# Wide cross attention: keys projected for four sequences at once, and the projections moved right behind the scores

## The reference

```
q = jnp.einsum('bne,ef->bnf', x, wq)      # x: 128 tokens x 160, normalized; f = 1280
k = jnp.einsum('bme,ef->bmf', ctx, wk)    # ctx: 77 tokens x 96
v = jnp.einsum('bme,ef->bmf', ctx, wv)
scores = jnp.einsum('bhnd,bhmd->bhnm', q, k) * SCALE    # 20 heads of 64
attn = jax.nn.softmax(scores, axis=-1)
out = jnp.einsum('bhnm,bhmd->bhnd', attn, v)
return jnp.einsum('bnf,fe->bne', out, wo) + bo
```

## Time and profile before

| | us |
|---|---|
| median of 3 runs | 3719.72 |
| lowest, highest run | 3706.51, 3859.67 |
| the profiled execution | 3714.61 |
| its span, first to last instruction | 3712.8 |
| mean granted clock of PE, as a share of 2.4 GHz | 0.989 |

### The profile page before, as it was taken

How to read it: one execution, slowest core, us unless ns; L and a number is a source line. 1 busy time by engine, 2 the same in 40 slices (tenths; PEclk the granted TensorE clock), 3 DMA queues, 4 the chain that set the end, 5 groups by cost and what they waited for, 6 DMA issues and landing times. The chain is left out here.

```text
span 3712.8 us, 98282 instructions
## 1 busy us (share of the span) xinstructions
PE 3613.0 (97%) x38023; PEld 3125.9 (84%) x38023; DVE 2301.5 (62%) x3916; ACT 2091.5 (56%) x5165; POOL 1260.7 (34%) x1279
## 2 busy tenths in 40 slices
PE   5999999999999999999999999899999999999999
PEld 4777777877887889889899888788888888888888
DVE  2788866665454666666666666556555555556554
ACT  2677777775344655555555555455555555555333
POOL 4333333332442333333333333333233322333442
PEclk8899999999999999999999999999999999999999
DMA  4343433321101000000000000100000000000000
GB/s 112 91 100 86 105 80 85 91 76 50 43 0 35 2 1 0 0 0 0 0 0 0 0 0 1 25 3 2 2 2 1 2 2 2 1 2 1 19 19 25
DMA packets 99546, 98.72 MB, mean 27 GB/s; under 512 B 31248, under 2 KB 74128, under 8 KB 99344
## 3 DMA queue, kind: packets, MB, share of 16 engines
q1 hardware_dynamic: 94224, 94.50, 9.8%
q0 software_dynamic: 5120, 1.35, 0.2%
HBM read 20.76 MB, written 5.24 MB: 7 GB/s over the span
## 5 line engine op out<-in xcount | busy, mean ns | idle before, releaser
L1181 POOL TENSOR_TENSOR a_probs<-a_probs,a_rsums 128x1024 f32<-128x1024 f32 x160 | 303.5, 1897 | 752.8 <-DVE a_rsums L1306 752.8
L1219 ACT ACTIVATE a_probs<-a_scores_banks,a_negmax 128x128 f32<-128x128 f32 x1280 | 366.7, 376 | 284.6 <-DVE a_negmax L1294 284.5
L1181 POOL TENSOR_TENSOR c_probs<-c_probs,c_rsums 128x616 f32<-128x616 f32 x160 | 204.2, 1276 | 758.2 <-DVE c_rsums L1306 758.2
L704 ACT ACTIVATE s_probs<-s_scoresT_banks 128x1024 f32<-128x1024 f32 (+1 forms) x320 | 327.2, 1022 | 194.3 <-PE s_scoresT_banks L877 192.1
L1219 ACT ACTIVATE c_probs<-c_scores_banks,c_negmax 128x77 f32<-128x77 f32 x1280 | 312.2, 334 | 197.4 <-DVE c_negmax L1294 197.3
L789 DVE TENSOR_REDUCE s_negmax<-s_scores_banks 128x8 f32<-128x1024 f32 (+1 forms) x320 | 322.4, 1007 | 150.2 <-PE s_scores_banks L859 146.2
L1287 DVE COPY c_outT<-c_out_bank 128x512 f32<-128x512 f32 x160 | 110.7, 692 | 367.1 <-PE c_out_bank L1466 307.0
L1287 DVE COPY a_outT<-a_out_bank 128x512 f32<-128x512 f32 x160 | 110.7, 692 | 293.1 <-PE a_out_bank L1466 239.9
L1635 DVE SCALAR_TENSOR_TENSOR f_hidden<-f_value_bank,bias,f_gate 128x512 f32<-128x512 f32 x160 | 120.1, 751 | 244.9 <-ACT f_gate L1610 243.0
L667 POOL DMA_DIRECT2D s_q_stack<-s_shift x160 | 93.5, 585 | 504.7 <-ACT s_shift L727 498.6
L1294 DVE TENSOR_REDUCE a_negmax<-a_scores_banks 128x4 f32<-128x512 f32 x320 | 206.2, 686 | 88.2 <-PE a_scores_banks L1365 88.2
(11 more groups left out here) (308 smaller groups left out, 10613.9 us busy)
## 6 DMA issues: line engine op xcount, KB each, us to landing
s_q_stack<-front SPq DMA_DIRECT2D x192, 160.0 KB, 3.3
s_k_stack<-front SPq DMA_DIRECT2D x96, 160.0 KB, 3.7
s_out<-s_heads SPq DMA_DIRECT2D x128, 80.0 KB, 2.5
s_k_stack<-front SPq DMA_DIRECT2D x96, 96.2 KB, 2.8
x_tokens<-in_x SPq DMA_DIRECT2D x16, 320.0 KB, 4.7
out_x<-x_tokens SPq DMA_DIRECT2D x16, 320.0 KB, 2.4
s_q_stack<-s_shift POOLq DMA_DIRECT2D x160, 8.0 KB, 2.7
s_ctx_in<-in_ctx SPq DMA_DIRECT2D x16, 115.5 KB
```

The costliest lines, as they stand in the source:

```text
L704: nc.scalar.activation(probs[i][0:NK, :, :], scoresT[0:NK, :, :], ACT.Exp).then_inc(s_exp, 1)
L1181: nc.gpsimd.tensor_tensor(probs[i][:], probs[i][:], rsums[(k - 1) % 2][:].unsqueeze(2).broadcast_to([P, UNIT, NK]), ALU.mult).then_inc(s_p ...
L1219: done = nc.scalar.activation(probs[i][:, h, :], scores[:, h // GROUP, h % GROUP * NK:(h % GROUP + 1) * NK], ACT.Exp, bias=negmax[k % 2][: ...
```

## The change

In `c1` alone:

- The keys get a tensor of their own, `keys_two`, 308 columns (4 x 77) per tile for the four sequences of a double. One tile of 128 rows is projected by three matmuls of 308 columns, once per double; before, the same tile was projected twice, by three matmuls of 154 columns for each pair.
- `KEY_TILES` says in which step which of the ten key tiles of the next double is projected: one tile in k = 6, 8, 9, 0, 2, 3, two tiles in k = 7 and k = 1, none in k = 4 and 5. All go through `odd_bank`.
- Both query tiles of a step go into `even_bank` (2 x 256 columns), and ACT copies them in one instruction of 512 columns (`query_out`).
- PE does the queries and keys right behind the scores (and the transposes of the norm), ahead of `transpose_step`; the values stay where they were, behind `output_step`.
- ACT does four exponentials, the query copy, four exponentials, the key copies (`keys_out`), the value copy.
- The context is transposed, cast and split once per double, for four sequences, in step k = 5: four transposes on PE right behind the scores, `ctx_high` of 308 columns at the head of ACT's step, `ctx_low` of 308 columns at the head of DVE's step. Its two loads are issued together in k = 0.

```
+        KEY_TILES = {6: (0,), 7: (1, 2), 8: (3,), 9: (4,), 0: (5,), 1: (6, 7), 2: (8,), 3: (9,)}
...
+        def keys_at(q, k):
+            double = q + (k + GROUPS) // BODY
+            return [(t, double, double * TILES + t) for t in KEY_TILES.get(k % BODY, ())] if cross and live(double, QUADS) else []
...
+            def query_out(q, k):
...
+                    act.wait_ge(s_qkproj, r + 1)
+                    nc.scalar.copy(qk[:, 2 * g:2 * g + 2, :], even_bank[:].rearrange("p (t n) -> p t n", t=2)).then_inc(s_qk, 1)
+
+            def keys_out(q, k):
+                for t, double, order in keys_at(q, k):
+                    act.wait_ge(s_kproj, order + 1)
+                    nc.scalar.copy(keys_two[:, t, :], odd_bank[:, 0:QUAD * NK]).then_inc(s_k, 1)
...
-                exponentials(q, k, 0, 6)
-                tile_out(q, k, 0)
-                exponentials(q, k, 6, 8)
-                tile_out(q, k, 1)
+                double = both_at(q, k)
+                if k == GROUPS and double is not None:
+                    act.wait_ge(crossing.s_T, 2 * double + 2)
+                    act.wait_ge(s_vproj, BODY * double)
+                    nc.scalar.copy(ctx_high[0:CTX_D, :], odd_bank[0:CTX_D, 0:QUAD * NKC]).then_inc(crossing.s_high, 2)
+                if cross:
+                    exponentials(q, k, 0, 4)
+                    query_out(q, k)
+                    exponentials(q, k, 4, 8)
+                    keys_out(q, k)
...
+                double = both_at(q, k)
+                if k == GROUPS and double is not None:
+                    dve.wait_ge(crossing.s_high, 2 * double + 2)
+                    nc.vector.tensor_tensor(ctx_low[0:CTX_D, :], odd_bank[0:CTX_D, 0:QUAD * NKC],
+                                            ctx_high[0:CTX_D, :].bitcast(F32), ALU.subtract).then_inc(s_ctx_split, 2)
                 if live(n - Y_LAG, WUNITS):
...
+            def project_queries(q, k):
...
+                if due(r):
+                    pe.wait_ge(s_v, r)
...
+                for i in range(2):
+                    cols = slice((2 * g + i) * P, (2 * g + i + 1) * P)
+                    last = products(nc, even_bank[:, i * KCOL:(i + 1) * KCOL],
+                                    [(qh[:, cols], hh), (qh[:, cols], hl), (ql[:, cols], hh), (qs[0:STACK, cols], hs)])
+                last.then_inc(s_qkproj, 1)
+
+            def project_keys(q, k):
+                for i, (t, double, order) in enumerate(keys_at(q, k)):
+                    if due(order):
+                        pe.wait_ge(s_k, order)
+                    if i == 0 and k % BODY in (3, 8):
+                        pe.wait_ge(done.s_y, 2 * (BASE + capped(pair_of(q, k) + 3, PAIRS)))
+                    if t == 0:
+                        pe.wait_ge(s_ctx_split, 2 * double + 2)
...
+                    products(nc, odd_bank[:, 0:QUAD * NK],
+                             [(kh[0:CTX_D, cols], ch), (kh[0:CTX_D, cols], cl), (kl[0:CTX_D, cols], ch)]).then_inc(s_kproj, 1)
+
+            def project_values(q, k):
...
+                pe.wait_ge(s_qk, r + 1 if cross else 2 * r + 1)
...
+                if cross:
+                    project_queries(q, k)
+                    project_keys(q, k)
                 transpose_step(q, k - T_LAG)
                 output_step(q, k - Y_LAG)
-                project(q, k, 0)
-                project(q, k, 1)
+                if not cross:
+                    project(q, k, 0)
+                    project(q, k, 1)
                 project_values(q, k)
                 values_step(q, k - T_LAG)
```

More of the change, by code:

```diff
@@ L463, in __init__ @@
         self.ctx_in = [sb(f"ctx_in{i}", [P, PAIR, CTX_D]) for i in range(2)]
-        self.high = [sb(f"ctx_high{i}", [P, PAIR * CTX_TOK], F32R) for i in range(2)]
-        self.low = [sb(f"ctx_low{i}", [P, PAIR * CTX_TOK], F32R) for i in range(2)]
+        self.high = sb("ctx_high", [P, QUAD * CTX_TOK], F32R)
+        self.low = sb("ctx_low", [P, QUAD * CTX_TOK], F32R)
         self.s_in = [m.semaphore(f"ctx_in{i}") for i in range(2)]
@@ L1074, in attention_wide @@
         s_qk = sem("qk_ready")
+        s_kproj = sem("kproj")
+        s_k = sem("k_ready")
         s_vproj = sem("vproj")
@@ L1364, in scores_step @@
                             rows, t, col = slice(dh * j, dh * j + dh), 2 * g + c, (2 * c + a) * NK
-                            last = nc.tensor.matmul(scores[:, j, col:col + NK], qk[rows, t, a * P:(a + 1) * P],
-                                                    qk[rows, t, KCOL + a * NK:KCOL + (a + 1) * NK], start=True, stop=True)
+                            if cross:
+                                keys = keys_two[rows, t, (k // GROUPS * PAIR + a) * NK:(k // GROUPS * PAIR + a + 1) * NK]
+                            else:
+                                keys = qk[rows, t, KCOL + a * NK:KCOL + (a + 1) * NK]
+                            last = nc.tensor.matmul(scores[:, j, col:col + NK], qk[rows, t, a * P:(a + 1) * P], keys,
+                                                    start=True, stop=True)
                 last.then_inc(s_scores, 1)
@@ L1490, in step @@
                     last.then_inc(crossing.s_T, 1)
+                double = both_at(q, k)
+                if k == GROUPS and double is not None:
+                    pe.wait_ge(s_k, TILES * double)
+                    for i in range(2):
+                        pe.wait_ge(crossing.s_in[i], 16 * (double + 1))
+                        for a in range(PAIR):
+                            last = nc.tensor.transpose(odd_bank[0:CTX_D, (i * PAIR + a) * NKC:(i * PAIR + a + 1) * NKC],
+                                                       crossing.ctx_in[i][0:NKC, a, :], m.ident[0:NKC, 0:NKC])
+                    last.then_inc(crossing.s_T, 2)
+                if cross:
+                    project_queries(q, k)
+                    project_keys(q, k)
                 transpose_step(q, k - T_LAG)
                 output_step(q, k - Y_LAG)
-                project(q, k, 0)
-                project(q, k, 1)
+                if not cross:
+                    project(q, k, 0)
+                    project(q, k, 1)
                 project_values(q, k)
```

84 lines of the change are left out of this document (52 added, 32 removed).

## The result

The changed kernel is slower: 3785.57 us in the median of five runs (3769.71 to 3835.72), beside 3741.65 for the kernel before on the same chip (3706.51 to 3859.67). The two medians also hold executions that a lower clock made longer; without those over 1.5% above the fastest of their kernel (one of five on either side) the ratio is 1.0167, 95% interval [1.0117, 1.0218]: about 62 us, 43 to 81, where +36 was forecast. That is slower beyond doubt, while a loss of 2% is neither shown nor excluded. The median lies inside the range of the forecast, near its upper end of 3792.

What follows compares the result with a forecast made beforehand. PE was taken to bound stage c1 (busy 198.4 of 200 us). Terms -19 - 12 - 6 + 53 + 8 + 12 = +36 us on 3714.6 gave 3750.6; predicted 3752 us, range 3718 to 3792.

Steps and rivals of the forecast that it cites:

- PE's own work: Queries and keys on PE in c1: 0.12 us saved per step over 155 steps, -19 us (ends -9 and -26).
- `ctx_low` wait gone: In s = 4 the odd bank no longer waits for `ctx_low`: 0.39 us in 30 pairs, -12 us.
- values' wait in s = 3 gone: In s = 3 the values no longer wait for the even copy: 0.2 us x 30, -6 us.
- second key tile: In k = 7 and k = 1 PE waits for ACT's copy of the first tile: 31 x 1.72 = +53 us (47 to 62).
- k = 3 and k = 8: Key tile waits for ACT's norm passes on the odd bank: 0.27 us in 30 steps, +8 us (0 to 12).
- k = 5: DVE waits for ACT's `ctx_high` ahead of `outT` and maxima, delaying the values: 15 x 0.8 = +12 us (8 to 18).
- falls of the clock: Rival: PE's clock falls behind the new waits, 1.5 us each; all 31 give +47 us, 3799; chance 0.10 of enough for 2%.
- its case of a third of the waits: A third of the 31 long waits draw a clock fall: 3768 us; chance of a third or so 0.17.
- the second tile hardly waits: Rival: ACT's first key copy is done early, wait under 0.55 us; with none 3698, or 3703 by the median; chance 0.06.
- the third: Rival: PE's savings at their upper end, small waits don't come: -26 - 12 - 6 + 50 = +6, 3721 us; chance 0.12.
- What was counted as hidden: Query copy (1.0 us of cover or more), key copy, ACT's copying per step and context loads: counted at nothing.
- The signs named in the prediction: In the changed trace: 1.7 us extra between key tiles 31 times, PE share about 94%, c1's granted clock 1.00, among others.

Runs made afterwards that it cites:

- all_three: Changed kernel, second key tiles and key tiles of k = 3, 8 behind the output projection, DVE's `ctx_low` behind the maxima; ratio 0.9915 to kernel before.
- context_later: Changed kernel with DVE's `ctx_low` in k = 5 moved behind `outT` and the maxima; c1 1113.6 us, against 1128.4 changed.
- filled_wait: Changed kernel with 14 idle matmuls of 256 columns ahead of the second key tile, keeping PE busy in the wait; c1 1104.2 us.
- all_three_narrow: all_three with each key tile projected by two times three matmuls of 154 columns; c1 1049.0 us, ratio 1.0016 to kernel before.
- move_alone: Kernel before with its projections moved behind the scores and transposes of norm and context, `ctx_low` behind the maxima; c1 1071.2 us, against 1058.9.
- late_second: Changed kernel with the second key tile of k = 1 and 7 behind the output projection; c1 1046.1 us, ratio 1.0013 to kernel before.
- early_copy: Changed kernel with ACT's copy of the first of two key tiles ahead of the last four exponentials; c1 1074.6 us.
- wide_old_place: Changed kernel with queries and keys put back behind the output projection, ahead of the values; c1 1193.8 us, 3865.53 in all.

## Why the prediction was wrong in its size

The sign and the places were right, and the size was short by half. The working's terms for c1 beside what the steps show:

| term | forecast, us | measured, us | from |
|---|---|---|---|
| PE's own work | -19 | -24 | one-tile steps 6.32 for 6.475 |
| `ctx_low` wait gone | -12 | -12 | k = 4 takes 5.89 = 6.32 less a tile, no wait in it |
| values' wait in s = 3 gone | -6 | -6 | no row of it is left |
| second key tile | +53 | +62 | 31 x (8.74 - 6.32 - 0.43) |
| k = 3 and k = 8 | +8 | +10 | all_three: 0.35 x 30 |
| k = 5 | +12 | +15 | context_later: 1.0 x 15 |
| sum without falls | +36 | +45 | |
| falls of the clock | 0 (a rival) | +24 | filled_wait |
| sum | +36 | +69 | c1: +69.5 |

The terms come out this near to c1 with some help: the 6.8 us fall in c1's first steps, worth 2.8, is in none of them, so the others are 2 or 3 us too high in sum.

**PE's work** came out at -0.155 a step, between the middle and the upper end of the prediction's range. all_three_narrow and move_alone say whence: from the width, not from the place. These 5 us more than forecast hid as much of what the waits and the clock cost beyond it.

**The second key tile is the term that was mis-sized.** The cause was right: late_second removes it, early_copy shortens it by what ACT's queue gives. The prediction had 1.72 from PE's readiness to its restart. Measured from the start of the scores, PE is ready at 2.54 (2.57 forecast); the first exponential starts at 1.76 (1.69), the key copy at 3.91 (3.82), and it takes 0.47, not 0.42; PE restarts at 4.44 (4.29), a wait of 1.90. The first matmul behind a pause then costs 0.10 more, a slow start that the prediction knew from its other terms and left out here. Together 1.99, against 1.72: +9 us with rounding, and at the upper end (2.0) of the bounds.

**The clock is the step that failed.** The prediction took c1's clock as 1.00 and kept the falls for a rival, on one pair of rows: no fall behind idle 1.74, a fall behind 1.88. That read as a threshold just above its own wait. There is none: in c1's body the same wait, 1.67 to 1.75 idle, drew a fall in 15 of 30 cases. The waits at the end of a1, which the change leaves alone, come out otherwise in the changed kernel's own trace than in the earlier trace rows. Timeline of PE there:

```profile
2381.60 1.09 PE L1546 MATMUL a_out_bank<-a_probsT,a_v 128*64 128x128 f32 x16 [1.88 <-DVE a_probsT L1355]
2382.63 1.16 PE L1418 MATMUL a_scores_banks<-a_qk 64*128 64x128 f32 x16
...
2387.64 1.09 PE L1546 MATMUL a_out_bank<-a_probsT,a_v 128*64 128x128 f32 x16 [1.75 <-DVE a_probsT L1355]
2388.67 1.99 PE L1418 MATMUL a_scores_banks<-a_qk 64*128 64x128 f32 x16
```

Behind 1.88 the scores take 1.16 here, behind 1.75 they take 1.99. Two rows of one execution that differ by 0.14 us can't tell a limit from chance. The rival's price of 1.5 us was right (1.6 measured); its case of a third of the waits, +16 us, came nearest, and it was half of them, +24. Had half the falls been in the forecast, it would have given 3752 + 24 = 3776, and with the longer wait 3785. The prediction's reason for few falls, three or more dense steps between two waits, is refuted: dense work ahead of the pause did not prevent a fall. The Trainium skill (TensorE: Matmul & The Clock Gate, Part 1) has the throttled clock as the default and activity as what releases it. The trace agrees that activity matters: filled_wait, with PE busy in the same 2.05 us, has no fall in the 30 steps that it fills.

**Small slips in the working.** By its own terms the forecast of the median is 3719.7 + 36 = 3756, not 3752. The cover of the query copy in a step with no key tile is 4.04 - 3.17 = 0.87 us, not 1.0 or more. Neither bears on the outcome. And its 1.72 us is counted from PE's readiness, while the 1.74 and 1.88 of the earlier trace rows are the profile's idle times, in which the measured wait of 1.90 shows as 1.75; set beside them, 1.72 was a longer wait than it should have been.

**k = 3, k = 8 and k = 5** are short by the same slow start and by 0.1 to 0.2 us of ACT and DVE: 0.35 and 1.0 instead of 0.27 and 0.8.

**The other rivals.** That the second tile hardly waits is refuted (wait 1.90, it needed under 0.55). Of the third, PE's savings nearly reached their upper end (-24 for -26), but the small waits came. What was counted as hidden stayed so: in steps with one key tile no wait for the query copy, the key copies or the context loads is seen, and wide_old_place shows what the cover is worth.

**The signs named in the prediction** came: two starts of key tiles 2.05 us apart (1.85 forecast), released by `c_keys`; PE's share at 93% (94%); 0.14 to 0.25 idle before the keys in k = 3 and 8 (0.3 forecast); the values of k = 5 released by `c_qk`. Two were wrong: the granted clock in c1, at 0.97 the sign named for its failure, and by a little the length of the wait.

## What to carry to other kernels

Where two producers fill one bank in turn, the second waits for the consumer's whole queue: count what stands there ahead of the copy, and put the second producer behind other work of its engine (moving three matmuls down in two of ten steps gave 82 us here). On an engine that bounds the kernel, price a wait of about 1.4 us or more, in this kernel, as the wait, plus the slow restart, plus a share of clock falls; don't read a limit for these from two rows. An edit that saves work per instruction should be tried apart from the reordering that comes with it: here the width was worth 29 us, and the place, tried by itself, cost 12.

## What the runs showed of the hardware

- The same wait of PE, 1.67 to 1.75 us idle in a dense stream, is followed by 1.2 GHz in 15 of 30 cases of c1's body and by 2.4 GHz in 15, in one execution of the changed kernel. Which ones differs between executions that differ in other steps only (context_later). Idle 1.43 drew one in 14 of 30 in wide_old_place, where PE also waits shortly in most other steps. Idle 0.80 to 0.88 drew none in 31 (early_copy), and neither did the long wait filled with matmuls.
- Short pauses in close order did draw one: at the start of c1 in early_copy, eight pauses of 0.25 to 0.85 us in some 14 us, none longer, end in a fall at 2375.7. What decides between fall and none is open.
- The fall doesn't show at once, and not always at the same place: 0.35 us after the restart in k = 1 of the changed kernel, 1.5 in k = 7, 0.7 to 2.1 in wide_old_place. So the slow work can stand well behind the wait.
- The falls have different lengths: 3.4 us in the body of the changed kernel, 6.8 in wide_old_place and at c1's start, and 102 in s0, where work that is the same in all these kernels ran at 0.93 on average in two executions (changed, all_three) and at 1.00 in the others. What sets the length is open.
- A matmul of 154 columns has 0.105 us to itself in a row of its kind, one of 256 columns 0.12, one of 308 columns 0.143. The first behind an idle time has 0.24 instead of 0.143.
